# Recommendation tower on one core: one table moved from one-hot lookup to gathers, and other waits for the gathers

## The chip, the cores and the metric

The kernel runs on one core of one Trainium2 chip. The metric is the device time in microseconds (us) of one execution. Before the change three runs took 477.92, 479.77 and 480.21 us; their median is 479.77 us.

## What is computed

A batch of 2048 samples, each with a dense vector of 128 numbers and 26 ids. Every id picks a row of 128 numbers from its own table (thirteen or more of the tables have 1000 rows, others 1250, 12500 or 125000). The 27 vectors of a sample are multiplied with each other, the 351 products of different pairs and the dense vector go through three layers.

```python
e = jnp.stack([tbl_0[ids[:, 0]], tbl_1[ids[:, 1]], ..., tbl_25[ids[:, 25]]], axis=1)
combined = jnp.concatenate([dense[:, None, :], e], axis=1)          # 2048 x 27 x 128
interactions = jnp.einsum('bfd,bgd->bfg', combined, combined)
z = interactions[:, iu, ju]                                         # 351 pairs i < j
h = jnp.concatenate([z, dense], axis=1)                             # 479
h = jnp.maximum(h @ W_top1 + b_top1, 0.0)                           # 512
h = jnp.maximum(h @ W_top2 + b_top2, 0.0)                           # 256
y = h @ W_top3                                                      # 1
```

## The kernel before

**Two ways to fetch a row.** Thirteen of the 1000-row tables are held in SBUF ("hot", NUM_HOT), split into a rounded part `hot_hi` and the rest `hot_lo`. VectorE builds a one-hot matrix by comparing ids with row numbers (`compare`, line 291), and TensorE multiplies it with both parts (`hot`, line 470: 16 matmuls a feature). The one-hot matrix of feature f lies in slot f modulo SLOTS (three slots), so that a compare waits for the matmuls of the feature SLOTS before it. The other thirteen ("cold") are fetched by GpSimd's indirect DMAs (line 266, one gather of 128 rows each) into `rows`, which also holds the dense vectors; TensorE turns them round (`transposes`, line 484).

**Turns and tiles.** A tile is 128 samples, a turn (s) is two tiles (t = 0 and 1), and there are eight turns. The hot features are done for both tiles of a turn at once, cold ones tile by tile, in four groups g: three, four, four and two gathers (the first group has the dense vectors beside them). One turn has 26 gathers.

**The order of TensorE** is written out by hand (`STEPS`): the thirteen hot features with the transposes of tile 0 between them, in the order hot 0, hot 1, rows 0, hot 2, rows 1, rows 2, hot 3, rows 3, hot 4 to 6 (a hot unit is two features, the last one); then half of layer 1 of the turn before (`1a`), the gram of tile 0 (`grams`, line 495: two halves of 64 small products each), rows 0 of tile 1, the other half of layer 1, rows 1 and 2, rows 3, layer 2 (line 552), the gram of tile 1, and layer 3 (line 560). ScalarE copies every unit from PSUM into `feats` (line 348), three banks in turn, and copies the first half of each gram; VectorE copies the second half (line 274). SyncE then moves the pairs (line 176, nine DMAs a tile), loads the next ids (line 189) and the dense vectors (line 195).

**The order of GpSimd**: turn by turn, tile by tile, group by group. Before a group it waits (1) until the same group of the tile before has been transposed, as `rows` has one buffer (`wait_rows_free`); (2) until all gathers of the group before have landed (`wait_landed`); and (3) ahead of group 2 of a turn's first tile, except in the first turn, until the second gram of the turn before is done (`gram_done[1]`).

**The first turn** also loads the hot tables and the weights (SyncE), rounds each table on ScalarE and takes the rest on VectorE (`rest`, line 278), so that VectorE does a compare and a rest for each feature. VectorE's later order in a turn: compares SLOTS to the last, the rest of the pairs (line 300), the first compare of the next turn, copy of the gram of tile 0, two more compares of the next turn, the rest of the dense vectors (line 307), copy of the gram of tile 1.

Of the kernel before, what the change touches and what calls it, by code (L numbers as in the profile page):

```python
# [5 lines left out]
NUM_HOT = 13  # L6


def dlrm_tower(nc, ids, dense, tables, ident, hot_ids, hot_tables, hot_rows, w1, b1, w2, b2, w3, out):
# [13 lines left out]
    NH = len(hot_tables)  # L23
# [7 lines left out]
    SLOTS = 3  # L31
# [11 lines left out]
    HOT = [list(range(f, min(f + 2, NH))) for f in range(0, NH, 2)]  # L43
# [16 lines left out]
    with ctx:  # L60
# [47 lines left out]
        dense_in = [sem(f"dense_in{t}") for t in range(2)]  # L108
        gathered = [[sem(f"gathered{t}_{g}") for g in range(NG)] for t in range(2)]
        raw_in = [sem(f"raw_in{f}") for f in range(NH)]  # L110
# [43 lines left out]
        def wait_rows_free(eng, s, t, g):  # L154

            if t == 1:
                wait_rows(eng, s, 0, g)
            elif s > 0:
                wait_rows(eng, s - 1, 1, g)

# [84 lines left out]
        def _(pool):  # L245
            def wait_landed(s, t, g):

                if g > 0:
                    t0, g0, s0 = t, g - 1, s
                else:  # L250
                    t0, g0, s0 = 1 - t, NG - 1, s - (t == 0)
                if s0 >= 0:
                    pool.wait_ge(gathered[t0][g0], 16 * sum(f > 0 for f in GROUPS[g0]) * (s0 + 1))

            pool.wait_ge(idx_in, 16)
            for s in range(TURNS):
                for t in range(2):
                    for g, features in enumerate(GROUPS):
                        wait_rows_free(pool, s, t, g)
                        wait_landed(s, t, g)  # L260
                        if s > 0 and t == 0 and g == 2:

                            pool.wait_ge(gram_done[1], 2 * s)
                        for f in features:
                            if f > 0:
                                pool.indirect_dma_start(  # L266
                                    out=rows[:, f, :], out_offset=None, in_=tables[f - 1],
                                    in_offset=bass.IndirectOffsetOnAxis(ap=idx[:, 2 * s + t, f - 1:f], axis=0),
                                ).then_inc(gathered[t][g], 16)

        @block.vector
        def _(dve):
# [39 lines left out]
            def turn(s, first, last):  # L312
# [18 lines left out]
                rest_of_dense(s)  # L331
                copy_gram(dve, copy, 1, s, 1, first)
# [122 lines left out]
        def _(pe):  # L455
# [5 lines left out]
            def hot(s, u, first):  # L461
                n, bank = place("hot", u)
                wait_bank(s, n)
                for f in HOT[u]:
                    pe.wait_ge(compared, NH * s + f + 1)
                    for part in (hot_hi, hot_lo):
                        if first:
                            pe.wait_ge(hot_rounded if part is hot_hi else hot_split, f + 1)
                        for c in range(HC):
                            mm = nc.tensor.matmul(psum[:, bank, (f % 2) * SB:(f % 2 + 1) * SB],  # L470
# [6 lines left out]
            def transposes(s, t, g):  # L477
# [3 lines left out]
                pe.wait_ge(gathered[t][g], 16 * sum(f > 0 for f in GROUPS[g]) * (s + 1))  # L481
# [190 lines left out]
```

## Time and profile before

| | us |
|---|---|
| median of 3 runs | 479.77 |
| the profiled execution, its own time | 484.05 |
| its span, first to last instruction | 482.2 |
| mean granted TensorE clock | 0.915 of 2.4 GHz |
| TensorE busy | 393.7 |
| VectorE busy | 298.3 |
| GpSimd busy | 204.5 |
| ScalarE busy | 159.8 |

The profile is of one execution. Times in its views are from the start of the span. An engine's line in a timeline gives start, duration, engine, line of the kernel, operation, what it writes and reads, how many instructions were merged, and in brackets how long the engine had been idle before, with what ended that. "issue" as the cause means that the engine waited for nothing that the profile shows. Matmul records overlap, and their ends are modelled, so starts are what to compare.

### The profile page before, as it was taken

To read this page: it belongs to the slowest core of one execution; us is meant where nothing else is said; L and a number is where in the kernel's file an instruction comes from. 1 tells how busy PE (TensorE), PEld (TensorE's weight loads), DVE (VectorE), ACT (ScalarE), POOL (GpSimd) and SP (SyncE) were. 2 spreads that over 40 slices of the span, in tenths; PEclk is the share of its full clock that TensorE was granted. 3 is DMA by queue.
4 is the path that set the end of the run, shared out by engine and by line. 5 is a ranking of instruction groups with operands and counts; after the bars stand their busy time and mean duration, and the time that the engine had idled before them with its cause. 6 is when DMAs were issued, how large, how long until landed. Compare 5 with 4: busy or idle time off the path is not lost.

```text
span 482.2 us, 14732 instructions
## 1 busy us (share of the span) xinstructions
PE 393.7 (82%) x6528; PEld 361.2 (75%) x6528; DVE 298.3 (62%) x199; ACT 159.8 (33%) x272; POOL 204.5 (42%) x212
## 2 busy tenths in 40 slices
PE   1856844899879987999879996997889986998847
PEld 1746733898769976898769983997779975997746
DVE  3994863696529934696639861893649843892210
ACT  2360452042433233333423352233323343234412
POOL 2432654345444554444543544454433544454000
PEclk9975975799889999899989998999979998999968
DMA  8997113121132112221122113211132113211000
GB/s 173 253 244 197 35 33 111 48 54 45 34 102 66 38 33 75 77 55 38 44 101 61 33 34 107 65 37 34 48 101 57 33 39 97 55 38 33 16 17 1
DMA packets 22249, 33.28 MB, mean 69 GB/s; under 512 B 5884, under 2 KB 15740, under 8 KB 22229
## 3 DMA queue, kind: packets, MB, share of 16 engines
q1 hardware_dynamic: 15388, 19.28, 15.3%
q0 software_dynamic: 6656, 13.64, 10.8%
q8 instruction: 13, 0.21, 0.2%
q10 hardware_dynamic: 186, 0.09, 0.1%
q14 instruction: 6, 0.05, 0.0%
HBM read 29.90 MB, written 0.01 MB: 62 GB/s over the span
## 4 chain that ended last, share of the span: by engine, by line
PE 70%; issue 11%; DMA 10%; POOL 4%; SPq 2%; DVE 1%; ACT 1%; POOLq 0%; ACTq 0%
PE psum L470 37%; PE psum L495 11%; DMA rows<-table,idx 8%; PE psum L552 5%; PE psum L484 5%; POOL rows L266 4%; PE psum L508 4%; PE psum L509 3%; PE psum L510 3%; SPq L176 2%; PE psum L560 2%; DMA pairs<-gram 1%; DVE gram L274 0%; DVE onehot L291 0%; DMA idx<-ids 0%
## 5 line engine op out<-in xcount | busy, mean ns | idle before, releaser
L266 POOL DMA_INDIRECT rows<-table,idx x208 | 204.3, 982 | 238.8 <-DMA rows<-table,idx 125.6
L291 DVE TENSOR_TENSOR onehot<-ids_b,psum 125x2048 fp32r<-125x2048 int16 x104 | 232.1, 2283 | 35.2 <-PE psum L470 25.2
L348 ACT ACTIVATE feats<-psum 128x512 f32<-128x512 f32 (+1 forms) x120 | 80.7, 709 | 182.5 <-PE psum L470 137.8
L470 PE MATMUL psum<-onehot,hot_hi 125*128 125x256 f32 x832 | 125.8, 295 | 16.2 <-ACT hot_hi L348 10.6
L470 PEld LDWEIGHTS psum<-onehot,hot_hi 125*128 125x128 f32 x832 | 110.4, 197 | 25.9 <-issue 18.6
L470 PE MATMUL psum<-onehot,hot_lo 125*128 125x256 f32 x832 | 118.4, 286 | 0.0
L274 DVE COPY gram<-psum 26x416 f32<-26x416 f32 x64 | 37.4, 584 | 116.8 <-PE psum L495 108.4
L470 PEld LDWEIGHTS psum<-onehot,hot_lo 125*128 125x128 f32 x832 | 108.6, 194 | 0.6
L495 PE MATMUL psum<-feats 128*26 128x26 f32 x4096 | 61.8, 202 | 45.0 <-issue 43.5
L495 PEld LDWEIGHTS psum<-feats 128*26 128x26 f32 x4096 | 51.3, 115 | 57.5 <-issue 54.0
L348 ACT ACTIVATE gram<-psum 26x416 f32<-26x416 f32 (+1 forms) x72 | 35.5, 493 | 57.4 <-PE psum L495 38.2
L484 PE MATMUL psum<-ident_sb,rows 128*128 128x128 f32 x224 | 34.2, 287 | 16.2 <-DMA rows<-table,idx 16.2
L484 PEld LDWEIGHTS psum<-ident_sb,rows 128*128 128x128 f32 x224 | 26.5, 147 | 17.6 <-DMA rows<-table,idx 16.9
L390 ACT ACTIVATE h<-psum,b_sb 128x256 f32<-128x256 f32 x44 | 18.4, 470 | 47.2 <-PE psum L510 24.7
L508 PE MATMUL psum<-pairs_hi,w_hi 126*128 126x256 f32 (+1 forms) x96 | 29.4, 306 | 5.2 <-DVE pairs L300 5.2
L509 PE MATMUL psum<-pairs,w_hi 126*128 126x256 f32 (+1 forms) x96 | 29.0, 302 | 0.0
L552 PE MATMUL psum<-h,w_sb 128*128 128x256 f32 x128 | 28.9, 379 | 0.0
L510 PE MATMUL psum<-pairs_hi,w_lo 126*128 126x256 f32 (+1 forms) x96 | 28.6, 298 | 0.0
L552 PEld LDWEIGHTS psum<-h,w_sb 128*128 128x128 f32 x128 | 23.6, 190 | 2.9
L508 PEld LDWEIGHTS psum<-pairs_hi,w_hi 126*128 126x128 f32 (+1 forms) x96 | 20.3, 211 | 5.5 <-DVE pairs L300 5.5
L509 PEld LDWEIGHTS psum<-pairs,w_hi 126*128 126x128 f32 (+1 forms) x96 | 20.3, 212 | 0.0
L510 PEld LDWEIGHTS psum<-pairs_hi,w_lo 126*128 126x128 f32 (+1 forms) x96 | 20.1, 210 | 0.0
(24 smaller groups left out, 128.5 us busy)
## 6 DMA issues: line engine op xcount, KB each, us to landing
lows<-table SPq DMA_DIRECT2D x13, 448.0 KB
ids_b<-hot_ids SPq DMA_DIRECT2D x8, 640.0 KB
rows<-table,idx POOLq DMA_INDIRECT x208
ids_b<-hot_ids SPq DMA_DIRECT2D x8, 192.0 KB
rows<-dense SPq DMA_DIRECT2D x16, 64.0 KB
lows<-w SPq DMA_DIRECT2D x1, 1024.0 KB, 25.0
lows<-table SPq DMA_DIRECT2D x13, 52.0 KB
pairs<-gram SPq DMA_DIRECT2D x16, 39.0 KB
```

What stands on the lines that cost most here:

```text
L266: pool.indirect_dma_start(out=rows[:, f, :], out_offset=None, in_=tables[f - 1], in_offset=bass.IndirectOffsetOnAxis(ap=idx[:, 2 * s + t, ...
L274: return nc.vector.tensor_copy(o, x)
L291: nc.vector.tensor_tensor(onehot[f % SLOTS][0:HP_ROWS, :, :], ids_b[0:HP_ROWS, f:f + 1, :].to_broadcast([HP_ROWS, HC, SB]), psum[0:HP_ROWS ...
L348: return nc.scalar.activation(o, x, ACT.Copy)
L390: nc.scalar.activation(dst[:, c, :], psum[:, bank, n * SB:(n + 1) * SB], ACT.Relu, bias=bias[:, c:c + 1]).then_inc(relu_out, 1)
L470: mm = nc.tensor.matmul(psum[:, bank, (f % 2) * SB:(f % 2 + 1) * SB], part[0:HP_ROWS, f, c, :], onehot[f % SLOTS][0:HP_ROWS, c, :], start= ...
L484: mm = nc.tensor.transpose(psum[:, bank, m * P:(m + 1) * P], rows[:, f, :], ident_sb[:, :])
L495: mm = nc.tensor.matmul(psum[32 * q:32 * q + NJ, GP[h], k * NJ:(k + 1) * NJ], feats[:, t, n, 0:NJ], feats[:, t, n, 1:NF], start=True, stop ...
L508: nc.tensor.matmul(o, w_hi, x_hi, start=(n == 0), stop=False)
L509: nc.tensor.matmul(o, w_hi, x_lo, start=False, stop=False)
L510: return nc.tensor.matmul(o, w_lo, x_hi, start=False, stop=(n == ZC))
L552: mm = nc.tensor.matmul(psum[:, HP[0], m * SB:(m + 1) * SB], w2_sb[:, c, m * P:(m + 1) * P], h1[:, c, :], start=(c == 0), stop=(c == C1 - 1))
```

## The change

Twelve tables are held in place of thirteen, so the thirteenth is gathered: a turn has 24 one-hot products (12 features for two tiles) in place of 26, and 28 gathers in place of 26 (groups of three, four, four and three). The hot units are five pairs and two single features. There are four one-hot slots; the fourth compare of the next turn is made ahead of the second copy of the gram. GpSimd waits for the second gram ahead of group 1 in place of group 2. Its wait for the group before counts all its gathers but the last (which has a semaphore of its own, on which TensorE waits too), and there is none in the first turn.

```diff
-NUM_HOT = 13
+NUM_HOT = 12
-    SLOTS = 3
+    SLOTS = 4
-    HOT = [list(range(f, min(f + 2, NH))) for f in range(0, NH, 2)]
+    HOT = [[f, f + 1] for f in range(0, NH - 2, 2)] + [[NH - 2], [NH - 1]]
...
         gathered = [[sem(f"gathered{t}_{g}") for g in range(NG)] for t in range(2)]
+        gathered_last = [[sem(f"gathered_last{t}_{g}") for g in range(NG)] for t in range(2)]
...
+        def wait_gathered(eng, s, t, g):
+
+            eng.wait_ge(gathered[t][g], 16 * (sum(f > 0 for f in GROUPS[g]) - 1) * (s + 1))
...
                 if g > 0:
-                    t0, g0, s0 = t, g - 1, s
-                else:
-                    t0, g0, s0 = 1 - t, NG - 1, s - (t == 0)
-                if s0 >= 0:
-                    pool.wait_ge(gathered[t0][g0], 16 * sum(f > 0 for f in GROUPS[g0]) * (s0 + 1))
+                    wait_gathered(pool, s, t, g - 1)
+                elif t == 0:
+                    wait_gathered(pool, s - 1, 1, NG - 1)
...
                         wait_rows_free(pool, s, t, g)
-                        wait_landed(s, t, g)
-                        if s > 0 and t == 0 and g == 2:
+                        if s > 0:
+                            wait_landed(s, t, g)
+                        if s > 0 and t == 0 and g == 1:
 
                             pool.wait_ge(gram_done[1], 2 * s)
...
-                                ).then_inc(gathered[t][g], 16)
+                                ).then_inc((gathered_last if f == features[-1] else gathered)[t][g], 16)
...
                 rest_of_dense(s)
+                if not last:
+                    compare(s + 1, 3, False)
                 copy_gram(dve, copy, 1, s, 1, first)
...
-                for f in HOT[u]:
+                for m, f in enumerate(HOT[u]):
...
-                            mm = nc.tensor.matmul(psum[:, bank, (f % 2) * SB:(f % 2 + 1) * SB],
+                            mm = nc.tensor.matmul(psum[:, bank, m * SB:(m + 1) * SB],
...
-                pe.wait_ge(gathered[t][g], 16 * sum(f > 0 for f in GROUPS[g]) * (s + 1))
+                wait_gathered(pe, s, t, g)
+                pe.wait_ge(gathered_last[t][g], 16 * (s + 1))
```

As written, `wait_landed` waits for nothing between the tiles of a turn (group 0 of tile 1), since neither of its branches holds there.

## Rows read from the trace of the kernel before

**Rows 1.** The page: busy time, share of the span and instructions of each engine.

```profile
PE 393.7 (82%) x6528; PEld 361.2 (75%) x6528; DVE 298.3 (62%) x199; ACT 159.8 (33%) x272; POOL 204.5 (42%) x212
```

**Rows 2.** Stretches, one a turn: us, busy of each engine, clock, DMA share, GB/s.

```profile
0.00:87.50 87.50, 47.34 (x748) 42.64 (x748) 56.28 (x36) 30.64 (x40) 37.63 (x37) 0.78 0.59 146
...
248.40:301.90 53.50, 48.05 (x817) 43.13 (x816) 35.68 (x25) 17.92 (x32) 25.52 (x27) 0.97 0.20 57
...
408.90:482.20 73.30, 60.09 (x885) 54.87 (x884) 30.79 (x24) 22.00 (x41) 17.79 (x19) 0.93 0.10 26
```

**Rows 3.** TensorE's timeline in the fifth turn.

```profile
248.42 1.21 PE L470 MATMUL psum<-onehot,hot_hi 125*128 125x256 f32 x8
...
256.72 1.22 PE L470 MATMUL psum<-onehot,hot_hi 125*128 125x256 f32 x8
...
276.30 0.28 PE L508 MATMUL psum<-dense_hi,w_hi 128*128 128x256 f32 x1
...
279.26 0.67 PE L495 MATMUL psum<-feats 128*26 128x26 f32 x40
...
290.62 0.52 PE L495 MATMUL psum<-feats 128*26 128x26 f32 x39
```

**Rows 4.** VectorE's timeline in the fifth turn.

```profile
254.38 19.87 DVE L291 TENSOR_TENSOR onehot<-ids_b,psum 125x2048 fp32r<-125x2048 int16 x9 [1.47 <-PE psum L470]
...
300.38 2.43 DVE L274 COPY gram<-psum 26x416 f32<-26x416 f32 x4 [10.37 <-PE psum L495]
```

**Rows 5.** Stretches of single grams, columns as in rows 2.

```profile
279.30:282.40 3.10, 2.64 (x257) 2.43 (x257) 0.00 (x0) 1.81 (x4) 0.39 (x1) 1.00 0.11 29
...
172.80:178.70 5.90, 3.63 (x259) 2.93 (x257) 0.00 (x0) 2.87 (x6) 2.36 (x3) 1.00 0.15 40
...
188.20:194.50 6.30, 3.54 (x258) 3.01 (x258) 0.00 (x0) 2.20 (x5) 1.89 (x2) 0.89 0.51 159
...
290.60:300.40 9.80, 5.04 (x258) 3.73 (x258) 0.02 (x1) 2.87 (x6) 4.05 (x5) 0.92 0.37 117
```

**Rows 6.** GpSimd's timeline in the fifth turn: gathers and the waits before them.

```profile
256.32 0.94 POOL L266 DMA_INDIRECT rows<-table,idx  x1 [3.31 <-DMA rows<-table,idx]
...
267.68 0.94 POOL L266 DMA_INDIRECT rows<-table,idx  x1 [2.32 <-DMA rows<-table,idx]
268.93 0.94 POOL L266 DMA_INDIRECT rows<-table,idx  x1 [0.31 <-issue]
...
301.14 0.94 POOL L266 DMA_INDIRECT rows<-table,idx  x1 [2.59 <-PE psum L495]
```

**Rows 7.** GpSimd's timeline in the first turn.

```profile
40.97 0.94 POOL L266 DMA_INDIRECT rows<-table,idx  x1 [7.67 <-DMA rows<-table,idx]
...
63.14 2.43 POOL L266 DMA_INDIRECT rows<-table,idx  x1 [0.30 <-issue]
...
71.64 0.94 POOL L266 DMA_INDIRECT rows<-table,idx  x1 [0.30 <-issue]
```

**Rows 8.** TensorE's timeline in the first turn.

```profile
40.75 1.11 PE L484 MATMUL psum<-ident_sb,rows 128*128 128x128 f32 x4 [9.90 <-DMA rows<-table,idx]
...
60.77 1.30 PE L495 MATMUL psum<-feats 128*26 128x26 f32 x132 [0.76 <-ACT feats L348]
...
74.32 0.69 PE L484 MATMUL psum<-ident_sb,rows 128*128 128x128 f32 x2 [3.98 <-DMA rows<-table,idx]
```

**Rows 9.** VectorE's timeline in the first turn.

```profile
11.68 2.28 DVE L291 TENSOR_TENSOR onehot<-ids_b,psum 125x2048 fp32r<-125x2048 int16 x1
...
15.01 2.28 DVE L291 TENSOR_TENSOR onehot<-ids_b,psum 125x2048 fp32r<-125x2048 int16 x1
...
45.32 2.29 DVE L291 TENSOR_TENSOR onehot<-ids_b,psum 125x2048 fp32r<-125x2048 int16 x1 [6.17 <-PE psum L470]
...
57.52 1.22 DVE L278 TENSOR_TENSOR hot_lo<-lows,hot_hi 125x1024 fp32r<-125x1024 f32 x1
62.46 2.29 DVE L319 TENSOR_TENSOR w_lo<-lows,w_hi 128x2048 fp32r<-128x2048 f32 x1 [3.72 <-ACT w_hi L348]
```

## The prediction

> **What bounds the kernel now.** I read the page's busy times first, then the turns one by one, and then each engine's timeline in the fifth turn and in the first. TensorE is busy 82% of the span and no other engine over 62% [rows 1]. The turns fall in three kinds [rows 2]: a first one of 87.5 us with TensorE busy 47.3 us at a granted clock of 0.78 of 2.4 GHz, six middle ones of (408.9 - 87.5)/6 = 53.6 us with TensorE busy 48 us at 0.97, and a last one of 73.3 us.
>
> In a middle turn the stages follow each other on TensorE [rows 3]. The one-hot stage takes 276.30 - 248.42 = 27.9 us, layer 1a 3.0, the first gram and what stands to the second gram 11.4, the second gram and layer 3 11.3. Two of these aren't paced by TensorE's own work. In the one-hot stage VectorE makes nine compares without a pause, 19.87/9 = 2.21 us each [rows 4], where TensorE needs about (8.30 - 0.6)/4 = 1.92 us a feature while its slots are full (four features and one group of transposes in 256.72 - 248.42 = 8.30) [rows 3]. And a gram takes 3.1 us where a third of a microsecond of one gather falls into it, 5.9 with three, 6.3 with two beside the load of the next ids (DMA share 0.51), 9.8 with five beside that load [rows 5], with the count of gathers beside GpSimd's busy time. Its instructions stall in steps: for each gather beside it (5.9 - 3.1)/3 = 0.9 us.
>
> In the first turn TensorE stood 9.90 us for the gathers of group 2 [rows 8]. GpSimd had paused 7.67 us before its next group [rows 7], against 2.3 to 3.3 us in a middle turn [rows 6]: landing is slow while the tables load, and each group pays it in full. That stall also held VectorE for 6.17 us [rows 9].
>
> **The change part by part, middle turns.** I count from G, the end of the second gram.
>
> One feature less takes 1.92 us from TensorE and 2.21 from VectorE; one more transpose a tile adds 0.1 each. The fourth slot moves one compare into VectorE's idle 10.37 us before the second gram's copy [rows 4], so that cost is nothing; were that gap gone, it would cost 2.2. Eight compares, 17.7 us, remain after the first feature. If the first of them starts as late as now (254.38 - 248.42 = 6.0 us in), the last feature ends at 6.0 + 17.7 + 2.1 = 25.8 us; if it starts at 2.2, TensorE is the bound: 12 x 1.92 + 2.0 for transposes = 25.0. I take 25.0, bounds 25.0 to 25.8: 2.9 us less than now. TensorE starts a turn 1.5 us after G (layer 3) and reaches rows 3 of tile 1 at G + 1.5 + 25.0 + 3.0 + 5.9 (first gram, still with gathers beside it) + 4.3 = 39.7.
>
> GpSimd now has 4 + 4 + 3 + 3 + 4 + 4 + 3 = 25 gathers behind G where it had 20. They start 0.8 us after G (300.38 to 301.14) [rows 4, 6], with a pitch of 1.25 us. The pauses get shorter: one was as long after three gathers as after four (2.3 us both times), so landing counts from each gather's own issue, and waiting for the last but one saves a pitch. Over the usual 0.31 us, the two pauses beside the pair DMAs and loads go from 3.0 to 1.75, the ordinary ones from 2.0 to 0.75; between the tiles there is none. So the last gather starts at 0.8 + 24 x 1.25 + 2 x 1.75 + 3 x 0.75 = 36.5, and TensorE can use it 2.7 us later (71.64 to 74.32) [rows 7, 8], at G + 39.2. That just meets TensorE's 39.7: no stall, and no slack. Group 2 of tile 0 lands at about 0.8 + 7 x 1.25 + 1.75 + 2.7 = 14.0 us, where TensorE wants it at 1.5 + 8.3 + 3.8 + 0.5 = 14.1; a stall there is 0 to 1 us.
>
> (The 4.3 is my share of the 290.62 - 282.4 = 8.2 us between today's grams: group 0's transposes, layer 1b's 24 matmuls and groups 1 and 2.) The rest of the 8.2, group 3 and layer 2, is 3.8 us, to 43.5. By then the three gathers that may run ahead of G have been issued (last start 36.5 + 0.75 + 3 x 1.25 = 41.0). The second gram so has the load of the ids beside it, which is 512 KB in place of 640, but at most the tail of one gather: 3.1 + 0.4 for the load (6.3 less 5.9; I allow 1.2) + up to 0.9. I take 4.5, bounds 3.1 to 7.6 (7.6 is today's mean of the six). The turn is 43.5 + 4.5 = 48.0 us, 5.6 less than 53.6. Six turns give 33.6; I take 2 off for the first of them, where ids and pair copies arrive late for VectorE: 31.6, bounds 12 to 40.
>
> **First turn.** VectorE's pitch of compare and rest is 15.01 - 11.68 = 3.33 us [rows 9], slower than TensorE's feature. Without pauses the 14 gathers of tile 0 are issued by 3.4 + 14 x 1.25 = 21 us and, at the slow landing of 8 to 9 us, in by 30; TensorE wants group 2 behind feature 5, at 11.7 + 5 x 3.33 + 2 = 30. The 9.90 us stall goes, and VectorE runs through: its last rest, now ending at 57.52 + 1.22 = 58.7, ends 6.2 (the wait), 3.3 (one feature) and 0.6 earlier, at 48.5. The first gram follows 2.0 us behind (60.77 now) [rows 8], at 50.5. Tile 1's gathers need no wait for landing either and are done by 46, so nothing waits for gathers as at 74.32 now (3.98 us) [rows 8]. What is late next is VectorE: 3.7 us for the rounding of the weights, then their rest, a compare and the first copy, 2.3 + 2.3 + 2.4, to 59. The second gram's second half starts there. At half clock (it was 12 us at 0.50 now, six of them stalls beside seven gathers) the gram ends at 62 to 66. I take 66 for the turn: 21.5 us less. Bounds 10 to 24: 10 if only VectorE's 6.2 + 3.3 come back.
>
> A rule speaks against unpaused gathers here. The gather at 63.14 took 2.43 us beside VectorE's rest of the weights, 62.46 to 64.75, where 0.94 is usual [rows 6, 7, 9]: such a subtract holds up GpSimd. The Trainium skill's SBUF page (Who interferes with whom) says that a `tensor_tensor` with two SBUF inputs contends with GpSimd's reads and infers that it doesn't stall descriptor generation; this trace differs. By the page tile 0 is issued by 21 us, by the row by about 26; rows 3 of tile 0 are wanted behind feature 7, at 37, so neither changes the sum.
>
> **Last turn.** Its end hangs on the first gram, through copies and pair DMAs; that comes 2.9 us earlier, less 1 for transposes and waits: 2, bounds 0 to 3.
>
> Sum: 482.2 - 21.5 - 31.6 - 2 = 427.1 us of span. The median of the runs lies 2.4 below the profiled span, so 424.7; I say 425. The bounds of all terms together are 482 - 24 - 40 - 3 = 415 and 482 - 10 - 12 = 460.
>
> **The rivals.**
> A (chance 0.15): the ids' load, not the gathers, stretches the second gram. It stays 7.6 us, a turn is 51.1, and the time is 425 + 6 x 3.1 = 444. For it: all long second grams have the load. Against: the gram with more gathers and the smaller share of DMA (0.37) took 9.8 us, that with fewer and 0.51 took 6.3 [rows 5].
> B (0.15): unpaused gathers land no sooner in the first turn, or the half clock holds there; it gains 10: 436. A and B together (0.06): 455.
> C (0.05): a pause doesn't shrink. Five pauses are then 12 us, rows 3 of tile 1 come at 0.8 + 30 + 12 + 2.7 = 45.5, the turn is 53.8 as now: 425 + 6 x 5.8 = 460, with up to 4 more at the end.
> D (0.04), slower than before: the clock. Group 2 and 3 of tile 0 now arrive just in time behind G. If those small stalls bring the half clock that the first turn shows (0.78 in the mean) [rows 2], half of the one-hot stage and layer 1, 15 us of work, take 15 more each turn: 425 + 7 x 15 = 530. It makes the kernel slower from 55/7 = 8 us of work at half clock a turn. Against: a gram of 5.9 us with stalls ran at 1.00 [rows 5].
> E (0.03): both stages do better, about 412.
>
> **How the numbers follow.** The forecast, 425, has 0.52. The range takes in A, B, both and the clearly shorter second gram: 414 to 456. A time within 0.5% of before (about what a measurement can tell from none) needs C with a lost first turn: 0.01. Slower, with D and its lesser kinds: 0.05. Faster: 0.94.
>
> **What would show it.** Right: the first turn about 66 us without a stall of TensorE before rows 1 and 2; 25 us from a turn's first one-hot matmul to layer 1a; a second gram of 4 to 5 us without gathers issued in it; ordinary pauses of GpSimd of 1.0 to 1.1 us; rows 3 of tile 1 wanted and landed within a microsecond. Wrong: pauses of 2.3 us (C), a second gram over 6 us with no gather in it (A), a first turn over 75 (B), one-hot stages at a clock of 0.5 (D), or TensorE waiting for rows in each turn.

## The result and the profile after

The changed kernel took 467.66 us (median of 4 runs, 465.62 to 469.38) where the kernel before took 479.99 (4 runs, 477.92 to 482.28): a ratio of 0.971, 95% interval 0.967 to 0.976. It is faster, by 12 us where 55 were predicted; 467.66 lies above the range of 414 to 456. The profiled execution took 466.8 us, its span is 465.0 us, its mean granted clock 0.923 of 2.4 GHz.

The page's busy times of the changed kernel, then its stretches: the first turn, a middle turn of the usual kind, the seventh turn and the last, with the columns of rows 2.

```profile
PE 383.8 (83%) x6416; PEld 351.7 (76%) x6416; DVE 280.5 (60%) x190; ACT 160.1 (34%) x271; POOL 220.8 (47%) x228
```

```profile
0.00:65.10 65.10, 38.97 (x734) 34.72 (x734) 54.08 (x35) 27.64 (x35) 37.19 (x35) 0.97 0.66 175
226.50:280.20 53.70, 45.54 (x803) 41.58 (x802) 33.04 (x23) 18.42 (x33) 26.85 (x28) 0.97 0.21 58
331.90:388.10 56.20, 49.32 (x804) 45.65 (x803) 33.22 (x23) 18.27 (x33) 26.40 (x28) 0.88 0.20 57
388.10:465.00 76.90, 59.33 (x871) 53.79 (x870) 27.18 (x23) 23.75 (x45) 23.57 (x25) 0.91 0.14 37
```

The first turn fell from 87.5 to 65.1 us [rows 2]. The six middle turns, (388.1 - 65.1)/6 = 53.8 us each, didn't fall at all from 53.6. The last turn is 3.6 us longer.

Inside the middle turns much moved. Here are the one-hot stages of two turns (from the first one-hot matmul to layer 1a) and the second gram that stands between the two, same columns.

```profile
226.50:255.40 28.90, 25.73 (x209) 24.69 (x209) 23.21 (x14) 8.75 (x15) 17.59 (x19) 1.00 0.27 77
327.90:331.00 3.10, 3.10 (x258) 2.86 (x257) 1.66 (x1) 0.84 (x2) 0.00 (x0) 1.00 0.10 26
331.90:370.60 38.70, 31.82 (x208) 29.95 (x208) 23.36 (x14) 9.82 (x16) 23.57 (x25) 0.82 0.25 71
```

The second gram is 3.1 us with no gather in it (POOL x0); the second grams of before took 6.3 to 9.8, two of them in [rows 5]. But the one-hot stage, 27.9 us before [rows 3], takes 28.8 to 38.7 us, 33.5 in the mean. The gain of the grams came back as a loss there. What it looks like on TensorE, in the seventh turn's timeline (form as in rows 3):

```profile
345.89 0.65 PE L493 MATMUL psum<-ident_sb,rows 128*128 128x128 f32 x4 [1.51 <-DMA rows<-table,idx]
347.64 0.79 ACT L356 ACTIVATE feats<-psum 128x512 f32<-128x512 f32 x1 [6.56 <-remote]
348.55 1.44 PE L478 MATMUL psum<-onehot,hot_hi 125*128 125x256 f32 x8 [2.01 <-DVE onehot L297]
...
356.25 0.71 PE L478 MATMUL psum<-onehot,hot_lo 125*128 125x256 f32 x4 [0.38 <-issue]
357.65 0.64 PE L478 MATMUL psum<-onehot,hot_hi 125*128 125x256 f32 x4 [0.69 <-issue]
359.06 0.64 PE L478 MATMUL psum<-onehot,hot_hi 125*128 125x256 f32 x4 [0.77 <-issue]
```

TensorE stops between one-hot matmuls for 0.4 to 0.8 us with "issue" as the cause, that is, for nothing that the profile shows. These are the steps in which the grams stalled before. Here is what TensorE waited for between 150 and 390 us (engine, what it was to work on and line, releaser: us in total, times, longest), changed kernel and then kernel before:

```profile
PE psum L478 <- issue: 11.9, 24, 1.1
PE psum L493 <- DMA rows<-table,idx: 4.0, 3, 1.9
PE psum L504 <- issue: 4.0, 9, 0.5
PE psum L478 <- DVE onehot L297: 2.0, 1, 2.0
...
PE psum L519 <- issue: 1.3, 2, 0.7
PE psum L517 <- issue: 0.6, 1, 0.6
```

```profile
PE psum L495 <- issue: 23.5, 42, 1.4
```

Before, the unexplained stops all lay in the grams (line 495). Now 24 of 36, and 11.9 of 17.8 us, lie in the one-hot products (line 478), 4.0 us in the grams (line 504) and 1.9 in layer 1 (lines 517 and 519). Their listed total is lower, yet more hangs on them. Matmuls seem to end late as well: ScalarE's copy at 347.64 had waited 6.56 us, and such copies start up to 8.9 us after the end recorded for their matmuls, against 2 us at most before.

The clock falls too. Of the six middle one-hot stages only the fifth turn's ran at a granted clock of 1.00; the others had 0.80, 0.87, 0.90, 0.90 and 0.82, so that 1.2 GHz held for some 8 us of a stage in the mean (an estimate from these shares). Before, five of the six had 0.98 or more. Here is the second turn's stage, then two stretches of the seventh turn's: TensorE with next to nothing to do, and the work some 12 us later.

```profile
65.10:99.60 34.50, 31.00 (x207) 29.91 (x208) 24.20 (x15) 9.68 (x15) 21.17 (x23) 0.80 0.27 76
345.00:348.00 3.00, 0.65 (x4) 0.42 (x4) 2.58 (x2) 0.36 (x1) 2.39 (x3) 1.00 0.15 44
360.00:366.00 6.00, 4.69 (x18) 3.91 (x18) 3.15 (x2) 1.93 (x3) 3.88 (x5) 0.50 0.16 44
```

So the 33.5 us of a stage are 29.4 us of recorded TensorE work and 4.2 us without any; the same work takes 24.8 us in a run whose stages all have 1.00 (below).

### The profile page after: what moved, and what is told of

Same layout as the page of the kernel before. It is cut to its first block, busy times and chain, and to the rows that moved or that the text cites. A ratio compares the mean times of both kernels' runs of the same rounds, so it can differ in the third digit from the quotient of the medians.

```text
span 465.0 us, 14516 instructions
## 1 busy us (share of the span) xinstructions
PE 383.8 (83%) x6416; PEld 351.7 (76%) x6416; DVE 280.5 (60%) x190; ACT 160.1 (34%) x271; POOL 220.8 (47%) x228
## 4 chain that ended last, share of the span: by engine, by line
PE 69%; issue 11%; another core or an unknown queue 5%; DVE 5%; DMA 4%; SPq 2%; ACT 2%; POOL 1%; ACTq 0%; POOLq 0%
PE psum L478 39%; PE psum L504 9%; PE psum L493 6%; PE psum L561 5%; PE psum L517 3%; PE psum L519 3%; PE psum L518 3%; DVE onehot L297 3%; SPq L183 2%; PE psum L569 1%; DMA rows<-table,idx 1%; DMA lows<-table 1%; ACT feats L356 1%; DVE hot_lo L284 1%
## 5 line engine op out<-in xcount | busy, mean ns | idle before, releaser
L272 POOL DMA_INDIRECT rows<-table,idx x224 | 220.6, 985 | 203.1 <-issue 73.0
L297 DVE TENSOR_TENSOR onehot<-ids_b,psum 125x2048 fp32r<-125x2048 int16 x96 | 216.4, 2283 | 63.9 <-remote 39.2
L478 PE MATMUL psum<-onehot,hot_hi 125*128 125x256 f32 x768 | 127.4, 307 | 33.1 <-issue 17.0
L356 ACT ACTIVATE feats<-psum 128x512 f32<-128x512 f32 (+2 forms) x120 | 81.7, 708 | 198.6 <-remote 120.5
L478 PEld LDWEIGHTS psum<-onehot,hot_hi 125*128 125x128 f32 x768 | 109.7, 207 | 44.1 <-issue 37.9
L478 PE MATMUL psum<-onehot,hot_lo 125*128 125x256 f32 x768 | 121.1, 300 | 9.9 <-issue 9.7
L504 PE MATMUL psum<-feats 128*26 128x26 f32 x4096 | 47.1, 195 | 17.2 <-issue 12.6
L504 PEld LDWEIGHTS psum<-feats 128*26 128x26 f32 x4096 | 42.9, 106 | 23.7 <-issue 19.4
L493 PE MATMUL psum<-ident_sb,rows 128*128 128x128 f32 x240 | 36.4, 289 | 6.3 <-DMA rows<-table,idx 4.0
L493 PEld LDWEIGHTS psum<-ident_sb,rows 128*128 128x128 f32 x240 | 29.0, 149 | 8.7 <-issue 8.1
L517 PE MATMUL psum<-pairs_hi,w_hi 126*128 126x256 f32 (+1 forms) x96 | 28.2, 294 | 6.9 <-DVE pairs L306 6.2
L519 PE MATMUL psum<-pairs_hi,w_lo 126*128 126x256 f32 (+1 forms) x96 | 27.9, 291 | 0.8 <-issue 0.7
L518 PE MATMUL psum<-pairs,w_hi 126*128 126x256 f32 (+1 forms) x96 | 28.1, 292 | 0.4 <-issue 0.4
L517 PEld LDWEIGHTS psum<-pairs_hi,w_hi 126*128 126x128 f32 (+1 forms) x96 | 19.0, 198 | 7.2 <-DVE pairs L306 6.4
```

The source lines that it names most:

```text
L272: pool.indirect_dma_start(out=rows[:, f, :], out_offset=None, in_=tables[f - 1], in_offset=bass.IndirectOffsetOnAxis(ap=idx[:, 2 * s + t, ...
L297: nc.vector.tensor_tensor(onehot[f % SLOTS][0:HP_ROWS, :, :], ids_b[0:HP_ROWS, f:f + 1, :].to_broadcast([HP_ROWS, HC, SB]), psum[0:HP_ROWS ...
L356: return nc.scalar.activation(o, x, ACT.Copy)
L478: mm = nc.tensor.matmul(psum[:, bank, m * SB:(m + 1) * SB], part[0:HP_ROWS, f, c, :], onehot[f % SLOTS][0:HP_ROWS, c, :], start=(part is h ...
L493: mm = nc.tensor.transpose(psum[:, bank, m * P:(m + 1) * P], rows[:, f, :], ident_sb[:, :])
L504: mm = nc.tensor.matmul(psum[32 * q:32 * q + NJ, GP[h], k * NJ:(k + 1) * NJ], feats[:, t, n, 0:NJ], feats[:, t, n, 1:NF], start=True, stop ...
```

## Experiments

Eighteen runs in seven series; a series (a "call" in the recorded expectations) was run together on one chip, with the kernel before beside it. "Changed" is the kernel after. One thing has to be known to read them. **The kernel before itself came out at two levels**, and all its runs of a series lay on the same one: medians of 467.6 to 469.4 us in four series (chips 10, 6, 8 and 9; single runs 459.2 to 472.7), and of 480 to 484 us in the first measurement and three further series (chips 6, 12, 3; single runs 477.9 to 487.8). Chip 6 shows both, so it isn't the chip's number alone. I call the first kind quiet series and the second stalling series, after what their profiles show. Every ratio is against the kernel before in the same series.

| kernel | series | us | before, same series | ratio (95%) | first / middle / last turn | one-hot | grams 1, 2 |
|---|---|---|---|---|---|---|---|
| before, first measurement | stalling | 479.99 | - | - | 87.5 / 53.6 / 73.3 | 27.6 | 5.7, 7.6 |
| changed, first measurement | stalling | 467.66 | 479.99 | 0.971 (0.967-0.976) | 65.1 / 53.8 / 76.9 | 33.5 | 3.8, 3.5 |
| before (one run) | quiet | 459.2 | 467.64 | - | 78.6 / 50.6 / 75.2 | 28.2 | 4.0, 3.4 |
| changed | quiet | 413.5 | 467.64 | 0.883 (0.876-0.890) | 64.9 / 46.3 / 69.0 | 26.3 | 3.6, 3.2 |

(Middle turns and stages are means of six; grams from their first matmul to the last one's recorded end. The profiled run of the kernel before in the quiet series is the fastest of its eight there; in the profile of the first experiment, whose middle turns are the same program, they took 52.1 us.)

### Four edits, one series (chip 10, quiet)

**Only the first turn's waits for landing taken away**, in the kernel before:

```diff
-                        wait_landed(s, t, g)
+                        if s > 0:
+                            wait_landed(s, t, g)
```

> The kernel before with one edit: GpSimd doesn't wait for landed gathers in the first turn; thirteen tables, three slots, all other waits as before. Theory 1 (the changed kernel's gain is the first turn alone: it ended at 65.1 us where before it ended at 87.5, while its six middle turns take 53.8 us, as before 53.6): the first turn ends at about 87.5 - 22.4 + 3.3 (one more table for VectorE) = 68, the middle turns stay at 53.6, the last at 73.3, about 460 us in all, faster than the changed kernel. Rival: the first turn's gain needs fewer tables or the fourth slot; then it ends at 75 or later and the time is over 467.

Measured: 456.17 against 469.11 us, ratio 0.971 (0.962 to 0.981); first turn 70.4 us (in the profiled run, which took 461.69). The kernel before has 78.6 in a quiet series, so this edit brings 8 us of its first turn and the other parts of the change 5 more.

**The changed kernel with the old, long waits for landing** in all turns but the first:

```diff
-                    wait_gathered(pool, s, t, g - 1)
-                elif t == 0:
-                    wait_gathered(pool, s - 1, 1, NG - 1)
+                    t0, g0, s0 = t, g - 1, s
+                else:
+                    t0, g0, s0 = 1 - t, NG - 1, s - (t == 0)
+                wait_gathered(pool, s0, t0, g0)
+                pool.wait_ge(gathered_last[t0][g0], 16 * (s0 + 1))
```

> The changed kernel with the landing waits of before in all turns but the first: GpSimd waits for all gathers of the group before, also between the tiles of a turn. Theory 2 (TensorE is starved while GpSimd issues gathers closely; pauses of 2.3 us let it catch up): the one-hot stage, 28.8 to 38.7 us in the changed kernel, falls to about 26 to 29, ScalarE's copies start at most 1 to 2 us behind the recorded end of their matmuls where they now start up to 8.9 behind, and rows 3 of tile 1 arrive later, so that a turn takes 52 to 54 us. Rival (the starving has to do with the one-hot slots or the gram wait, not with the pauses): the one-hot stage stays over 31 us, and the later rows come on top: turns of 56 or more.

Measured: 488.28 us, ratio 1.040 (1.029 to 1.050): slower than before, with middle turns of 56.8 us. In TensorE's timeline of one of them:

```profile
283.69 0.90 PE L495 MATMUL psum<-ident_sb,rows 128*128 128x128 f32 x3 [6.10 <-DMA rows<-table,idx]
284.38 5.84 PE L563 MATMUL psum<-h,w_sb 128*128 128x256 f32 x16
```

TensorE stands 6.1 us for rows 3 of tile 1, and layer 2 behind it takes 5.84 us where it takes 3.6 otherwise; the granted clock was 0.5 from 278.6 to 288.9 us, so it fell 1.0 us into that wait, after 3.10 us of idling ahead of the transposes at 276.96. That is rival C's price (a chain of 25 gathers with long pauses: a turn of 53.8, with the pause between the tiles that this kernel also has again about 55.8), and rival D's mechanism on top of it: waits bring half clock, and the work behind them pays.

**The changed kernel without gathers after the first turn** (the rows of the first turn stay in place; TensorE's and GpSimd's waits for the gathers are left out with them; shown is the gathers' line):

```diff
-                        for f in features:
+                        for f in features if s == 0 else ():
```

> The changed kernel without any gather after the first turn (left out: the gathers and TensorE's waits for them; the transposes read the first turn's rows), so its output isn't the reference's. If gathers are what starves TensorE: one-hot stage 25 us, grams 2.4 to 3.1, a turn of about 25 + 3 + 2.4 + 8.2 + 3.1 + 1.5 = 43 to 44 us at a granted clock of 1.00. If the stalls come from TensorE's own instruction stream or from the clock: turns stay over 48 us with stalls in the one-hot stage.

Measured: 394.11 us, middle turns 43.4, one-hot stage 24.9, first gram 2.5. My 25.0 for the one-hot stage is what TensorE and VectorE need when nothing disturbs them, and a gram with nothing beside it takes 2.4 us.

**The wait for the second gram at group 2**, where it was before, all else as changed:

```diff
-                        if s > 0 and t == 0 and g == 1:
+                        if s > 0 and t == 0 and g == 2:
```

> The changed kernel with GpSimd's wait for the second gram ahead of group 2, as before, in place of group 1. Theory 2 (stalls follow the gathers wherever these are): group 1's four gathers fall beside layer 2 and the second gram, which goes from 3.1 to about 6 or 7 us, and the one-hot stage, with four gathers less behind the gram, falls by as much or more; turns of 52 to 54 us. Rival (the wait moved to group 1 makes the one-hot stage's rows late, and this is the loss): the one-hot stage falls to 26 to 28 and a turn to 50 or 51, about 450 us in all.

Measured: 405.78 us, ratio 0.862 (0.853 to 0.870), the fastest version of all. I had no run of the changed kernel in this series, and 467.66 less 405.78 sets one series against another: 62 us for one wait. So the changed kernel itself was run again.

### The changed kernel and the one before again (chip 6, quiet)

> The changed kernel itself, word for word, on the chip of this call. The run with the gram wait at group 2 took 405.8 us beside 469.1 of the kernel before, and TensorE stalled neither in its grams nor in its one-hot stages. Theory 3 (the place of the gram wait decides: at group 1 it starves the one-hot stage): 97.1% of the kernel before, some 456 us if that takes 469, with one-hot stages of 29 to 38 us. Rival (the stalls of TensorE's dispatch belong to the chip or the execution, and the one of the first profiles had them): one-hot stages of about 25 to 26 us, turns of 44 to 46, some 410 us.

> The kernel before itself, for a profile on the same chip. Theory 3: grams of 5 to 10 us beside gathers, as in the first profile. Rival (chip or execution): grams of 3 to 4 us beside gathers, and a time some 11 us lower than the 480 of the first profile, the loss then lying in the gathers' landing.

Measured: the changed kernel took 413.5 us, ratio 0.883 (0.876 to 0.890), not 467.66. The kernel before took 459.2 us in its one profiled run (its seven others in this series lie between 462.7 and 471.8). Stretches of the changed kernel here (columns as above): first turn, a middle turn, its one-hot stage, its two grams, last turn.

```profile
0.00:64.90 64.90, 40.59 (x735) 36.03 (x735) 54.26 (x35) 27.38 (x35) 37.00 (x35) 0.97 0.64 175
251.60:296.00 44.40, 42.32 (x804) 39.98 (x803) 32.75 (x23) 17.75 (x32) 26.62 (x29) 1.00 0.26 70
251.60:277.20 25.60, 24.63 (x208) 24.40 (x208) 22.43 (x13) 8.73 (x14) 17.14 (x18) 1.00 0.29 74
280.20:283.10 2.90, 2.77 (x258) 2.50 (x257) 0.00 (x0) 1.86 (x4) 1.58 (x2) 1.00 0.28 68
292.40:295.20 2.80, 2.80 (x258) 2.63 (x258) 0.73 (x1) 1.05 (x3) 0.00 (x0) 1.00 0.13 41
342.70:411.70 69.00, 55.35 (x871) 50.83 (x870) 26.41 (x22) 22.80 (x43) 24.29 (x25) 0.95 0.14 36
```

The first turn is the same as in the first measurement; the whole difference of 53.3 us of span lies in the middle turns, 6 x 7.5, and the last, 7.9. A gram with two gathers beside it now takes 2.9 us, one without 2.8. The stops put down to "issue" are gone from TensorE's waits between 150 and 390 us, which begin with:

```profile
PE psum L493 <- DMA rows<-table,idx: 8.4, 7, 1.9
PE psum L493 <- ACT feats L356: 5.6, 5, 1.3
```

ScalarE's copies start no later than 1.2 us after the end recorded for their matmuls. The kernel before in this series shows no such stop either after its third turn, and from there its first grams, with three or four gathers beside them, take 3.8 to 4.0 us.

**No wait for the gram at all**, all else as changed (the `pool.wait_ge(gram_done[1], 2 * s)` and its condition left out):

> The changed kernel without any wait of GpSimd for the second gram. Theory 3, taken further (every gather behind the gram costs in the one-hot stage): as fast as with the wait at group 2 or faster, 400 to 406 us, the second gram at 4 to 5 us. Rival (the wait at group 2 is a good middle): group 2's gathers fall into the second gram, which takes 6 us or more, 415 us or more.

Measured: 406.89 us, ratio 0.867 (0.861 to 0.876). The second gram takes 4.8 us for 3.2, and the stretch from the start of layer 1b to layer 2 takes 4.3 for 5.5.

### Changed, gram wait at group 2, and no gathers side by side (chip 8, quiet)

> The changed kernel, word for word, once more, on the chip of this call. Theory 4 (TensorE's dispatch stalls belong to the chip or to where the program is placed on it, as the first profiles had them and two later ones not): either about 0.88 of the kernel before with one-hot stages of 25 to 27 us, or about 0.97 with stages of 29 us or more and idle time of TensorE put down to issue in turns from the third on; nothing between. Rival (stalls come and go between executions on one chip): some of the four executions near 413, others near 467.

> The changed kernel with the gram wait at group 2, beside the changed kernel on the same chip. Theory (group 1 ahead of the gram takes four gathers off GpSimd's chain, 5.0 us, and what it adds to the second gram is 1.3 us): 1 to 3% faster than the changed kernel if the chip has no dispatch stalls; with them, faster in the one-hot stage and slower in the second gram, within 2% of the changed kernel. Rival (GpSimd's chain doesn't bound): the same time within 0.5%.

> The changed kernel without gathers after the first turn (left out: the gathers and TensorE's waits for them, so its output isn't the reference's), on the chip of this call. If the chip has the dispatch stalls and the gathers bring them: no stalls after the second turn, about 394 us as before. If the stalls are TensorE's own on such a chip: over 410 us. On a chip without stalls: 392 to 396 us, which tells only what the gathers still cost.

Measured: 412.52 us, 0.881 (0.873 to 0.890); 405.73 us, 0.868 (0.859 to 0.877); 393.68 us. So all gathers after the first turn together cost the changed kernel 19 us in a quiet series (3.1 us in a middle turn, 46.2 to 43.1), and the place of the gram wait 6.8 us. With the wait at group 2 the second gram has two or three gathers beside it and takes 4.0 to 4.4 us (5.2 in the second turn):

```profile
241.60:245.60 4.00, 3.79 (x258) 3.21 (x258) 1.66 (x1) 1.04 (x3) 1.76 (x2) 1.00 0.34 83
```

In return GpSimd has four gathers less behind the gram, and rows 3 of tile 1 come in time: from the start of layer 1b to layer 2 it is 4.2 us, where the changed kernel takes 5.5 and TensorE waits for rows again and again (8.4 us in 7 waits, above). A middle turn is 44.7 us with the wait at group 2 and 46.2 with it at group 1; six times the difference, with 1.1 us more in the first turn and 1.1 less in the last, are the 9.2 us between the two profiled spans, of which the medians show 6.8.

### The two halves of the change (chip 9, quiet)

**Waits only**: the changed kernel with thirteen tables, three slots and the old pairs of features.

```diff
-NUM_HOT = 12
+NUM_HOT = 13
-    SLOTS = 4
+    SLOTS = 3
-    HOT = [[f, f + 1] for f in range(0, NH - 2, 2)] + [[NH - 2], [NH - 1]]
+    HOT = [list(range(f, min(f + 2, NH))) for f in range(0, NH, 2)]
-                if not last:
-                    compare(s + 1, 3, False)
```

**Tables and slots only**: the changed kernel with the long waits as in the second experiment, in the first turn too (`if s > 0 or t > 0 or g > 0:`), and the gram wait at group 2.

> The changed kernel, word for word, on the chip of this call. If dispatch stalls are rare and the first measurement had them: 0.88 of the kernel before once more, 411 to 415 us. If they are common: 0.97 and 465 us in one call out of a few.

> The new waits alone: thirteen tables, three slots and VectorE's order as before, with GpSimd's waits as in the changed kernel. Theory (table, slot and waits each pay only together, since GpSimd's chain and the one-hot stage stand side by side): the one-hot stage stays 26.6 to 28 us, paced by VectorE; GpSimd's chain of 23 gathers behind the gram gets 2.5 us shorter; rows never late; turns of about 46.3 + 1.9 = 48 us and a first turn of 68, about 428 us. Rival (the waits bring all of it): 415 us or less.

> Twelve tables and four slots alone, all of GpSimd's waits as before (also in the first turn, and for the gram at group 2). Theory: TensorE's one-hot stage falls to 25 us, but 28 gathers with pauses of 2.3 us and more take 28 x 1.25 + 8 x 2.2 + the wait for the gram = 54 us or more, and rows 3 of tile 1 are what TensorE waits for: turns of 52 to 55 us, 470 to 485 us in all, no gain or a loss. Rival (TensorE's own work is the bound): turns of 48 us and 440 us.

Measured: changed 410.28 us, 0.880 (0.872 to 0.887); waits only 423.53 us, 0.908 (0.901 to 0.916); tables and slots only 477.42 us, 1.022 (1.013 to 1.031). Moving a table to the gathers makes the kernel some 2% slower as long as GpSimd's pauses stay long; TensorE's first entry in the list of waits (150 to 390 us) says why:

```profile
PE psum L495 <- DMA rows<-table,idx: 22.1, 5, 6.0
```

With the short waits, the same table and slot are worth 13 us (423.53 to 410.28): in the profiles 4.0 us in the first turn, 1.1 in each middle turn (28.1 to 26.2 us in the one-hot stage, less 1.1 us of waiting for rows 3) and 1.2 in the last. The parts depend on each other; the two ratios multiplied don't give the whole (0.908 x 1.022 = 0.928 against 0.880).

### Stalling series again (chips 6, 12, 3)

The same chip number as in the second series, but the kernel before took 483.63 us:

> The changed kernel, word for word, on the chip of this call, a fourth time. If dispatch stalls are what one chip in a few has: 465 us with them, else 409 to 415 us. TensorE's idle time put down to issue beside one-hot matmuls and grams from the third turn on: 14 us in the first profile of it, none in the later ones.

> The changed kernel without gathers after the first turn (left out: the gathers and TensorE's waits for them, so its output isn't the reference's). Beside a stalling run of the changed kernel it tells whether the gathers bring the stalls (then 394 us and none) or not (over 410 us). On a chip without stalls: 391 to 396 us.

Measured: changed 475.99 us (two runs, 0.990, 0.965 to 1.014), with TensorE's stops at line 478 back:

```profile
PE psum L478 <- issue: 15.6, 28, 2.6
PE psum L504 <- issue: 3.8, 8, 0.5
```

Its six middle one-hot stages ran at granted clocks of 0.86, 0.89, 0.85, 0.94, 0.90 and 0.82. Without gathers the kernel took 394.06 us, as in the quiet series (394.11 and 393.68; one run each). A one-hot stage of it, and a whole middle turn (a later one):

```profile
157.80:182.60 24.80, 24.71 (x209) 24.48 (x209) 23.03 (x14) 9.87 (x16) 0.00 (x0) 1.00 0.14 44
283.90:325.90 42.00, 41.91 (x803) 40.04 (x802) 32.68 (x23) 17.94 (x33) 0.00 (x0) 1.00 0.11 31
```

Of 42.0 us TensorE is busy 41.9, at full clock. So the stalls need the gathers: a series that costs the changed kernel 63 us more than a quiet one costs this kernel nothing.

Where the stalls fall, three kernels of the changed family:

> The changed kernel with the gram wait at group 2, hoped for beside a kernel before of some 480 us (the state with dispatch stalls). Theory (a gather in flight holds up TensorE's dispatch wherever it falls, so that moving gathers moves the loss): 465 to 480 us, the second gram 6 us or more, one-hot stages of 29 us or more. Rival (what starves the one-hot stage is the run of eight gathers behind the gram): one-hot stages of 25 to 27 us and 440 us or less. Beside a kernel before of 468 us: 406 us once more, which tells neither.

> The changed kernel with the landing waits of before in all turns but the first, hoped for beside a kernel before of some 483 us (the state with dispatch stalls). Theory (the shorter pauses starve TensorE's one-hot stage): stages of 26 to 30 us as in the kernel before, turns still long for GpSimd's chain, 490 us. Rival (a stall comes with each gather, whatever the pause): one-hot stages of 32 us or more and over 510 us.

> The new waits with thirteen tables and three slots, beside a kernel before of some 483 us. It took 0.908 without the stalls. Theory (stalls follow the gathers behind the gram, and this kernel has 23 of them there in place of 25, at the same pauses): 0.97 to 1.00 of the kernel before, one-hot stages of 30 us or more. Rival (VectorE's pace in the one-hot stage leaves TensorE slack that takes the stalls up): 0.93 to 0.95, stages of 28 us.

| kernel, stalling series | us (before) | middle turn | one-hot | grams 1, 2 |
|---|---|---|---|---|
| gram wait at group 2 | 451.71 (483.81), 0.936 (0.931-0.941) | 51.4 | 27.8 | 4.0, 6.9 |
| long pauses | 478.86, one run (484.18) | 55.5 | 28.5 | 9.4, 4.1 |
| waits only | 484.66 (484.18), ten runs: 472.93, the rest 483.1 to 493.0 | 55.4 | 37.1 | 2.8, 3.3 |
| changed, fifth series | 475.99 (483.63) | 54.9 | 34.3 | 4.1, 3.5 |

One stretch of each of the first three (columns as above): the second gram with the wait at group 2, the first gram with long pauses, the one-hot stage with the waits only.

```profile
269.50:276.10 6.60, 3.90 (x258) 3.35 (x258) 1.68 (x2) 2.29 (x5) 1.73 (x2) 0.74 0.46 132
```

```profile
264.20:273.50 9.30, 4.23 (x258) 3.37 (x258) 0.00 (x0) 2.88 (x6) 4.13 (x5) 0.94 0.14 38
```

```profile
292.90:331.30 38.40, 33.02 (x223) 30.56 (x223) 25.71 (x15) 10.09 (x16) 21.74 (x23) 0.87 0.26 69
```

Against the same kernel in a quiet series, the stalls add this to a middle turn:

- changed: 8.1 to the one-hot stage (26.2 to 34.3), 0.3 to the second gram; the turn grows by 8.7 (46.2 to 54.9).
- waits only: 9.0 to the one-hot stage (28.1 to 37.1), nothing to the grams; the turn grows by 8.6.
- gram wait at group 2: 2.8 to the one-hot stage (25.0 to 27.8), 2.5 to the second gram (4.4 to 6.9); the turn grows by 6.4 (45.0 to 51.4).
- long pauses: 0.1 to the one-hot stage, 6.6 to the first gram (2.8 to 9.4), 1.3 to the second; the turn doesn't grow but falls by 1.3 (56.8 to 55.5), since a late gram only shortens TensorE's wait for rows 3.
- before: nothing to the one-hot stage, 1.8 and 4.1 to the grams; the turn grows by 3.0 (50.6 to 53.6; by 1.5 from the 52.1 of the first experiment), since the wait for rows 3 gets shorter here too.

The first and the third differ in nothing but the gram wait, though they were run in different series. So **with the short pauses it is the wait at group 1 that moves stalls from the second gram into the one-hot stage**, and makes them dearer there. Neither of its companions does it alone: all 25 gathers stand behind the second gram in the kernel with long pauses too, which has 28.5 us in the one-hot stage; and the kernel with the wait at group 2 has the short pauses, and 27.8. The dearer part is half clock: TensorE's recorded work in a stage is 29.4 us in the mean in both stalling profiles of the changed kernel, and 26.0 with the wait at group 2, whose stages had granted clocks of 0.91 to 1.00; the time without work is 4.2 and 4.9 us against 1.8.

The first gram of the changed kernel is hardly longer in the mean (4.1 for 3.6), because in most turns its gathers are over before it starts: the one-hot stage got so long that 22 to 25 gathers fell beside it, where it is 18 in a quiet series (in the fifth turn 19). Where they still meet, the gram stalls as it did before, here partly at half clock. Here are the first grams of the fifth and the sixth turn in the fifth series:

```profile
264.70:273.70 9.00, 5.16 (x258) 4.03 (x258) 0.00 (x0) 2.27 (x5) 3.54 (x4) 0.63 0.14 36
324.60:327.00 2.40, 2.40 (x258) 2.34 (x258) 0.00 (x0) 1.87 (x5) 0.00 (x0) 1.00 0.00 0
```

What stays open is what the stall is, why whole series have it or not, and why the one-hot stages of the kernel before, with 14 or 15 gathers beside each, show no stop in a stalling series. I looked at two candidates in the profiles: between 150 and 390 us the instruction queues carry one or two packets in either kind of series, and a gather's packets of 4 KB take 216 to 232 ns in the median in both. Neither separates them.

## Why the prediction missed its range

Against the predicted span of 427.1 us the profiled one is 37.9 longer: first turn -0.9, middle turns +33.2, last turn +5.6. Point by point:

- **First turn**: predicted 66, measured 65.1 (64.9 to 66.0 in the other runs of this kernel). TensorE waited for no rows there (at tile 1 it stood once, 1.38 us before 57.31, put down to "issue"); B falls. Gathers did take 1.78 us rather than 0.94 beside VectorE's subtracts (27.08 below), at no cost, and the second gram began at 59.94, whose second half I had starting at 59:

```profile
27.08 1.78 POOL L272 DMA_INDIRECT rows<-table,idx  x1 [0.30 <-issue]
```

```profile
59.94 3.14 PE L504 MATMUL psum<-feats 128*26 128x26 f32 x246 [1.54 <-ACT feats L356]
```

  That gram was over with the turn, in 5 us and not the 12 of before. The Trainium skill's page SBUF — State Buffer (Who interferes with whom) infers that a `tensor_tensor` doesn't stall descriptor generation; as in rows 7 and 9, the gather's 1.78 us says otherwise.

- **Pauses**: predicted 1.05, and 2.05 beside the pair DMAs. Measured 1.07, 1.06 and 1.14, and 1.92 and 1.46 for the long ones; C falls as a mechanism, though its time of 53.8 us a turn is what came out. GpSimd's timeline in the seventh turn:

```profile
338.67 0.94 POOL L272 DMA_INDIRECT rows<-table,idx  x1 [1.92 <-issue]
...
344.81 0.94 POOL L272 DMA_INDIRECT rows<-table,idx  x1 [1.46 <-DMA rows<-table,idx]
...
353.07 0.94 POOL L272 DMA_INDIRECT rows<-table,idx  x1 [1.07 <-issue]
...
358.82 0.94 POOL L272 DMA_INDIRECT rows<-table,idx  x1 [1.06 <-issue]
...
364.64 0.94 POOL L272 DMA_INDIRECT rows<-table,idx  x1 [1.14 <-issue]
...
367.14 0.94 POOL L272 DMA_INDIRECT rows<-table,idx  x1 [0.30 <-issue]
```

  The last gather behind the gram started 367.14 - 331.0 = 36.1 us after the gram's end (327.90 and 3.10 us, above); 36.5 was predicted. That rows 3 would just be met, with no slack, was right to about a microsecond: in quiet series TensorE waits some 1.2 us for them. (The 20 gathers that I counted behind the gram of before were 19; no sum used it.)

- **Second gram**: 4.5 predicted, bounds 3.1 to 7.6; measured 3.5. A falls: with the ids' load and no gather it is 3.1 to 3.3 us from the third turn on.

- **One-hot stage**: 25.0 predicted, bounds 25.0 to 25.8; measured 33.5. **This is the step that failed**, with 8.5 us a turn. Of these, 4.2 us are time without work on TensorE, and nearly all the rest is its work getting longer at half clock (29.4 us recorded for 24.8, with 1.2 GHz for some 8 us a stage). My reading of the grams, 0.9 us for each gather beside one, took the stalls for a cost that belongs to a gather beside a gram. The quiet series show that this cost is small there, 2.4 us without gathers, 2.9 with two and 3.5 with three, and that more than half of the 0.9 belonged to something that comes in some series only. Taking the gathers out of the gram didn't take it out of the turn; it fell into the one-hot stage, where it cost more than in the gram. I had bounded that stage by its own work (compares and matmuls) alone; the trace of before did show 14 or 15 gathers beside it and no stop. The bound should have held the other case: the stalls that leave the grams may go where the gathers go, up to 42 stops in 240 us.

- **First gram**: 5.9 "still with gathers beside it", measured 3.8, 2.1 us a turn in the other direction. This overlap was wrong too: the one-hot stage ran so long that in five of the six turns at most one gather was left beside the gram (2.4 us with none), and in the fifth turn, with three, it took 6.2. With 1.0 less from the second gram, the 8.5 above and 0.4 in the rest of the turn, the turn is 5.8 us over the 48.0.

- **Rival D** (small waits bring half clock in the one-hot stage), which had a chance of 0.04, is about half of the miss: five of the six stages ran at 0.80 to 0.90, which cost some 4 us a turn. Its price of 15 us a turn didn't come, and its cause, late groups 2 and 3 of tile 0, is the smaller part: 4.0 us of waits for rows in 240 us, beside 17.8 us of stops put down to "issue".

- **Last turn**: 71.3 predicted, 76.9 measured in the stalling series, 69.0 in a quiet one. Its one-hot stage has the same fault as the others, 33.1 us for 27.9 before.

In the quiet series the ratio comes out near the predicted one: 425/479.77 = 0.886 was predicted, 0.880 to 0.883 measured three times. That is luck. There the middle turn is 46.3 us for 48.0 (one-hot +1.3, first gram -2.3, waiting for rows 3 +1.2, second gram -1.3, the rest -0.6), and the change gains less than was forecast in the first turn (78.6 to 64.9, 13.7 us for 21.5) and more in the last (6.2 for 2). The prediction's numbers were for a series whose kernel before took 480 us, and the 410 to 413.5 us of the quiet series lie below the range, where rival E had 412.

## What to carry over

A stop that the profile puts down to "issue" has no known owner, and an edit that takes its neighbours away may as well move it as remove it: bound the stage to which the neighbours go with the same stops in it. Time the kernel before beside each version, and once a version without the suspected work (394 us with and without stalls here): across series this change read as 1.0%, 2.9% or 12%. Where work moves to an engine that waits in pauses, shorten the pauses first (the moved table with its slot cost 2.2% alone and brought 13 us with short pauses), and of this family keep the changed kernel with its gram wait at group 2, 405.7 us in quiet series and 451.7 in a stalling one, faster than both kernels in each kind. When an engine's stage comes out long, read its granted clock stage by stage before naming the waits as the whole cause.

## What the runs showed of the chip that I had not expected

- The same program takes 410 to 414 us in some series and 468 to 476 in others on a lone core, and the kernel before 468 or 480 to 484. The changed kernel's first turn shows no mark of it (64.9 to 66.0 us in all).
- In the series with stalls TensorE stops about 0.5 us at a time, every 0.74 us or so, in streams of gram matmuls while GpSimd's gathers run (the medians of 56 stops between 90 and 395 us in the first profile of the kernel before). Among one-hot matmuls the stops are less regular: 0.35 and 0.42 us in the median and 1.1 and 1.4 us apart in the two profiles of the changed kernel. VectorE's and GpSimd's own instructions keep their durations (2.28 us a compare, 0.94 a gather).
- A wait of 6.1 us for rows, with 3.1 us of idling shortly before it, was followed by layer 2 at a granted clock of 0.5, 5.84 us for 3.6. That is 2.2 us behind the wait. The Trainium skill's page TensorE: Matmul & The Clock Gate (HAM oscillation — how this bites in real kernels) says that gaps between matmuls bring the clock down in the middle of a kernel; this trace agrees.
